# A fused attention and three-convolution kernel: mask products ahead of the first convolution, a longer TensorE loop, and the third convolution's end on ScalarE and GpSimd

## The chip, the cores and the metric

One core of a Trainium2 chip runs the whole program. The metric is the device time of one execution in microseconds. Three timed executions of the kernel before took 2295.17 (the median), 2292.28 and 2295.76 us.

## The reference, cut to what matters

The input x is [8, 128, 128, 64] in float32 (NHWC). A local attention over the 3x3 neighbourhood of each pixel comes first, then three 3x3 convolutions with ReLU, and the sum of the attention's output and the convolutions' output is returned:

```python
q = einsum('bhwd,de->bhwe', x, Q_P)
k = einsum('bhwkd,de->bhwke', stk, K_P)        # stk: the 9 shifted views of x
v = einsum('bhwkd,de->bhwke', stk, V_P)
alpha = softmax(einsum('bhwke,bhwe->bhwk', k, q) * mask)
t = x + einsum('bhwk,bhwke->bhwe', alpha, v)
t_in = t
t = relu(conv(t, ff1_kernel) + ff1_bias)        # 64 -> 64
t = relu(conv(t, ff2_kernel) + ff2_bias)        # 64 -> 128
t = relu(conv(t, ff3_kernel) + ff3_bias)        # 128 -> 64
return t_in + t
```

## The kernel before, in words

Images are worked on in 4 pairs (PAIRS), an image in each half of the 128 partitions. An image is cut into 16 bands of 8 rows (BANDS). One **step** works on one band at several stages at once: attention of band b, and the three convolutions of the bands behind it. A pair has 17 steps, k = 0 to 16; step k = 15 has no attention part (att is False), since the next pair's first band is taken up in k = 16. There are 68 steps, and the tail behind them finishes the last piece of the third convolution.

**Attention of a band.** TensorE makes r = (Q K^T) x for all 16 patches of 8x8 pixels (r_product, L367 to L374, into mix_bank and proj_bank). ScalarE copies r to rq (keep_r, L639). For each half of the patches TensorE makes scores: first four bfloat16 matmuls put the window mask (0 or a very negative number) into score_banks (L387), then 16 small products per half add the scores on top (L393). VectorE takes the maxima (max_scores, L756), ScalarE the exponentials (L627), VectorE scales by the reciprocal sum (scale, L762 and L765), TensorE turns the probabilities (turn, L405), ScalarE copies them (keep_turned, L644), TensorE multiplies them with x (mix, L420), ScalarE copies the result (keep_y, L634), TensorE applies V (v_product, L432), and VectorE adds x and writes tf (add_x, L776).

**Convolutions.** Each is done in a transformed domain with four streams, in which the column direction costs four products for two outputs. VectorE prepares the inputs from the ReLU's output (transform, L789, L790, L794), TensorE multiplies (conv1 L442, conv3_tile L484, begin2, go_on2 and end2 L500), ScalarE copies one of the two middle streams out of PSUM (keep_m2, L663, and keep_u2, L651), VectorE forms sum and difference with the other (middle and middle1, L819 to L833) and then adds the two outer streams (outer, outer1, outer3: L866, L841, L857). ScalarE adds bias and ReLU for convolutions 1 and 2 (L679, L693). For the third convolution VectorE does all of it: the bias goes in with middle (L819, L820), and finish (L783) takes the maximum with 0 and adds the kept attention output, in one scalar_tensor_tensor. SyncE then stores the band (store, L317).

**Order.** The order on every engine is written out by hand as a fixed sequence of calls per step. The functions schedule (for SyncE, ScalarE and VectorE) and the loop at L610 (for TensorE) run it: a loop over the pairs holds k = 0 and k = 1 written out, then an inner loop, then the last steps written out. TensorE's inner loop has 12 rounds (k = 2 to 13), and k = 14, 15, 16 are written out behind it. GpSimd has no loop: it only zeroes buffers and prepares the weights of the third convolution at the start. At the end of a step TensorE runs end2(G, k, 2) and end2(G, k, 3); the second has a wait for the next band inside it (await_band, L362), in every step but k = 14. The next step opens with r_product and then the inner half of conv1, which waits for outer of the second convolution's odd rows (L866) on VectorE, for dt_done, and for the small copy of dt.

**SyncE** issues all transfers in a fixed order per step: the copy of dt, loads of xs and xc, copies of dodd and deven, the store, the load of xk behind a wait for mix, the load of xr behind add_x, six copies into kept, and the copies of duh and dul behind the last tile of the second convolution.

Of the kernel before, what the change touches and what calls it, by code (L numbers as in the profile page):

```python
# [61 lines left out]
def pairs3(k):  # L62
    return (2, RP) if k == 1 else (0, 2) if k == 0 else (0, RP)
# [11 lines left out]
def build(nc, x_bands, x_keys, qt2, kt, vbd, w1, w2, w3, b1, b2, b3, window, eye, eye16, out):  # L75
    with ExitStack() as ctx:
# [6 lines left out]
        def sem(name):  # L83
            return ctx.enter_context(nc.semaphore(name))
# [91 lines left out]
        dve_read = sem("dve_read")  # L176
        sum_done = sem("sum_done")
        relu_done = sem("relu_done")
        dt_done = sem("dt_done")
        du_high = sem("du_high")  # L180
        du_low = sem("du_low")
# [175 lines left out]
        def _(pe):  # L357
# [20 lines left out]
                if half:  # L378
                    pe.wait_ge(probt_ready, b * 2 + 1)

            def scores(b, half):
                banks = [score_banks[:, n, 0:GROUP * KEYS].rearrange("q (a n) -> q a n", n=KEYS) for n in range(2)]
                mask = window_sb[:].rearrange("q (o n) -> q o n", o=1).broadcast_to([128, GROUP, KEYS])
                for n, swap in ((0, False), (1, True)):
                    for rows in (LOWER, UPPER):
                        to = (UPPER if rows is LOWER else LOWER) if swap else rows
                        nc.tensor.matmul(banks[n][to], eye16_sb[rows, rows], mask[rows], start=True, stop=False)  # L387
                for a in range(GROUP):
                    for n, swap in ((0, False), (1, True)):
                        patch = half * HALF + n * GROUP + a  # L390
                        for rows in (LOWER, UPPER):
                            to = (UPPER if rows is LOWER else LOWER) if swap else rows
                            mm = nc.tensor.matmul(banks[n][to, a], rq[rows, patch],  # L393
                                                  xc[rows, :, patch * PATCH:patch * PATCH + HALO],
                                                  start=False, stop=a == GROUP - 1)
                            if a == GROUP - 1:
                                mm.then_inc(scores_done, 1)
# [152 lines left out]
            r_product(0)  # L550
            await_r(0, 0)
            hold(score_banks[:, 0])
            scores(0, 0)
            await_prob(0, 0)
            hold(score_banks[:, 0])
            turn(0, 0)
            await_r(0, 1)
            hold(score_banks[:, 0])
            scores(0, 1)
            mix(0, 0)  # L560
            await_prob(0, 1)
# [11 lines left out]
            def step(G, k, b, att):  # L573
                if att:
                    r_product(b)
                conv1(G, k, b, False, att)
                if att:
                    scores(b, 0)
                conv1(G, k, b, True)
                conv3_tile(G, k, 0)  # L580
                conv3_tile(G, k, 1, (lambda: await_prob(b, 0)) if att else None)
                if att:
                    turn(b, 0)
                conv3_tile(G, k, 2, (lambda: await_r(b, 1)) if att else None)
                if att:
                    scores(b, 1)
                conv3_tile(G, k, 3)
                if att:
                    mix(b, 0)
                begin2(G, k, 0)  # L590
                go_on2(G, k, 0)
                begin2(G, k, 1, (lambda: await_prob(b, 1)) if att else None)
                if att:
                    turn(b, 1)
                go_on2(G, k, 1)
                end2(G, k, 0)
                end2(G, k, 1)
                if att:
                    mix(b, 1)
                begin2(G, k, 2, (lambda: await_y(b)) if att else None)  # L600
                if att:
                    v_product(b)
                go_on2(G, k, 2)
                begin2(G, k, 3)
                go_on2(G, k, 3)
                end2(G, k, 2)
                next_band = None if k == BANDS - 2 else b if k == BANDS - 1 else b + 1
                end2(G, k, 3, None if next_band is None else lambda: await_band(next_band))

            with pe.Fori(0, PAIRS) as p:  # L610
                g0, b0 = p * STEPS, p * BANDS
                step(g0, 0, b0 + 1, True)
                step(g0 + 1, 1, b0 + 2, True)
                with pe.Fori(0, BANDS - 4) as h:
                    step(g0 + h + 2, 2, b0 + h + 3, True)
                step(g0 + (BANDS - 2), BANDS - 2, b0 + (BANDS - 1), True)
                step(g0 + (BANDS - 1), BANDS - 1, b0 + BANDS, False)
                step(g0 + BANDS, BANDS, b0 + BANDS, True)
            for j in range(4):
# [3 lines left out]
        def _(act):  # L623
# [60 lines left out]
            def relu_conv2(G, k, which, behind=0):  # L684
# [6 lines left out]
                if k == BANDS and which == EVEN:  # L691
                    nc.scalar.copy(to[:, 1, :, 1:1 + W], zeros[:, 0])
                nc.scalar.activation(to[:, lo:hi, :, 1:1 + W], sums[which][:, lo:hi], ACT.Relu,  # L693
                                     bias=bias[:, 1:2]).then_inc(relu_done, 1)

            def u_high(G, k, part):
                act.wait_ge(d_done[CONV1], parts(G, part))
                if part == 0:
                    act.wait_ge(u_kept, G * 32 + 32)
                streams, n = PARTS[part], new_slots(CONV1, k)  # L700
                nc.scalar.copy(duh[:, 1:n + 1, streams], du[:, 0:n, streams]).then_inc(du_high, 1)
# [15 lines left out]
            def step(G, k, b, par, att):  # L717
                if att:
                    keep_r(b, 0)
                if k:  # L720
                    relu_conv2(G, k - 1, ODD, 1)
                    relu_conv2(G, k - 1, EVEN, 1)
                if att:
                    keep_r(b, 1)
                keep_u2(G, k)
                if att:
                    exps(b, 0)
                    exps(b, 1)
                keep_m2(G, k, CONV3)
                relu_conv1(G, k)  # L730
                if att:
                    keep_turned(b, 0)
                u_high(G, k, 0)
                u_high(G, k, 1)
                if att:
                    exps(b, 2)
                    exps(b, 3)
                if att:
                    keep_y(b, 0)
                    keep_turned(b, 1)  # L740
                keep_m2(G, k, ODD)
                keep_m2(G, k, EVEN)
                if att:
                    keep_y(b, 1)
                if k == BANDS:
                    relu_conv2(G, k, ODD)
                    relu_conv2(G, k, EVEN)

            schedule(act, step)
            keep_m2(ALL_STEPS, 0, CONV3)  # L750

        @block.vector
        def _(dve):
# [13 lines left out]
            def add_x(k, b, par, i):  # L767
# [6 lines left out]
                v = (proj_bank, mix_bank)[i][:].rearrange("c (a r s) -> c r a s", r=RP, s=PATCH)  # L774
                x = xr[:, :, i].rearrange("c r (a s) -> c r a s", s=PATCH)
                nc.vector.tensor_tensor(o, v, x, ALU.add).then_inc(t_ready, 1)  # L776

            def finish(G, k, b):
                lo, hi = pairs3(k)
                dve.wait_ge(dve_read, outer_read(G, CONV3))  # L780
                dve.wait_ge(carried, carries(k, b))
                o = sums[CONV3][:, lo:hi]
                nc.vector.scalar_tensor_tensor(o, o, 0.0, kept[:, k % 2 if k else 1, lo:hi], ALU.max,  # L783
                                               ALU.add).then_inc(out_ready, 1)

            def transform(to, src, slots, part, done):
                if part == 0:
# [21 lines left out]
            def middle(G, k, which):  # L809
                lo, hi = pairs(which, k)  # L810
                bank = conv_banks[:, bank_of(which, 1)].rearrange("c (s i w) -> c s i w", i=2, w=WT)
                m1, m2 = bank[:, lo:hi], m2_sb[:, which % 2, lo:hi]
                left, right = (sums[which][:, lo:hi, :, n::2] for n in range(2))
                dve.wait_ge(act_read, act_reads(G, which))
                dve.wait_ge(tile_done, filled(G, which, 1))
                if which == CONV3:
                    dve.wait_ge(sent, G * 16 + 16)
                if which == CONV3:
                    nc.vector.scalar_tensor_tensor(left, m1, bias[:, 2:3], m2, ALU.add, ALU.add)  # L819
                    nc.vector.scalar_tensor_tensor(right, m1, bias[:, 2:3], m2, ALU.add,  # L820
                                                   ALU.subtract).then_inc(dve_read, 1)
                else:
                    nc.vector.tensor_tensor(left, m1, m2, ALU.add)
                    nc.vector.tensor_tensor(right, m1, m2, ALU.subtract).then_inc(dve_read, 1)

            def middle1(G, k):
                lo, hi = pairs1(k)
# [75 lines left out]
            def step(G, k, b, par, att):  # L903
# [32 lines left out]
                    scale(b, 2)  # L936
                    scale(b, 3)
                u_low(G, k, 1)
                finish(G, k, b)
                middle(G, k, ODD)  # L940
                middle(G, k, EVEN)
                if att:
# [10 lines left out]
            schedule(dve, step)  # L953
            middle(ALL_STEPS, 0, CONV3)
            outer3(ALL_STEPS, 0)
            finish(ALL_STEPS, 0, PAIRS * BANDS + 1)

        @block.gpsimd
        def _(pool):
# [8 lines left out]
                nc.gpsimd.memset(credits[:, i:i + 1], 0.0).then_inc(credit, n)  # L968
            pool.wait_ge(w_in, 80)
            whole_weights(nc.gpsimd, pool.wait_ge, raws[3], w3f, half3, w3_stage).then_inc(w_ready, 1)  # L970


# [79 lines left out]
```

## Time and profile before

| | |
|---|---|
| profiled execution, its own time | 2292.98 us |
| its span | 2291.0 us |
| granted TensorE clock, mean | 0.987 |
| PE busy | 2184.0 us (95%) |
| VectorE (DVE) busy | 1894.3 us (83%) |
| ScalarE (ACT) busy | 1132.7 us (49%) |
| GpSimd (POOL) busy | 15.5 us (1%) |

Busy time is a union over an engine's instructions. PE is TensorE's matmuls and PEld its weight loads, which overlap the matmuls. Every matmul on float32 appears as two records. A busy PE is not PE at its peak, since matmuls are pipelined and their ends are modelled. The chain of waits goes back from the last instruction to what released each one, so what stands in it sets the end.

### The profile page before, as it was taken

The page shows a single profiled execution, that of the slowest core. Times are in us where ns is not written, and L with a number is a line of the kernel's source. Part 1 is how long each engine was busy: PE and PEld are TensorE (multiplying, and loading weights), DVE is VectorE, ACT ScalarE, POOL GpSimd, SP SyncE. Part 2 cuts the span into 40 slices and gives each one's busy share as a digit, 9 for nine tenths or more (in the row PEclk, how much of TensorE's full clock was granted, in tenths as well). Part 3 has the DMA queues.
Part 4 walks back from the last instruction along what each step waited for, and adds up shares of the span by engine and source line. Part 5 has one row for each costly group of instructions (what it writes and reads, how often), then busy time and mean ns, then how long its engine had stood idle before and what let it go on. Part 6 is the DMA issues. An engine that isn't in the chain of part 4 may idle for free.

```text
span 2291.0 us, 63881 instructions
## 1 busy us (share of the span) xinstructions
PE 2184.0 (95%) x24401; PEld 1222.3 (53%) x24401; DVE 1894.3 (83%) x2850; ACT 1132.7 (49%) x3108; POOL 15.5 (1%) x24
## 2 busy tenths in 40 slices
PE   4999999999899999999989999999988999999998
PEld 2555555554455555555455555555545555555554
DVE  4888888888688888888768888888876888888885
ACT  2555455553455455455345555555434555554542
POOL 2000000000000000000000000000000000000000
PEclk8999999999999999999999999999999999999999
DMA  5454544554355444544345445445534544454444
GB/s 130 140 145 142 166 141 136 155 153 136 103 155 168 145 140 147 161 145 132 118 145 154 136 154 156 145 132 166 151 117 111 168 146 142 139 166 145 141 147 124
DMA packets 291284, 328.75 MB, mean 144 GB/s; under 512 B 89300, under 2 KB 223252, under 8 KB 284564
## 3 DMA queue, kind: packets, MB, share of 16 engines
q1 hardware_dynamic: 291164, 327.17, 48.2%
q8 instruction: 73, 1.20, 0.2%
q14 instruction: 47, 0.39, 0.1%
HBM read 152.50 MB, written 33.82 MB: 81 GB/s over the span
## 4 chain that ended last, share of the span: by engine, by line
PE 87%; DVE 6%; issue 3%; ACT 1%; DMA 1%; SPq 1%; DVEq 0%; ACTq 0%
PE conv_banks L484 29%; PE conv_banks L500 24%; PE conv_banks L442 17%; PE mix_bank L420 5%; PE score_banks L393 4%; DVE work L866 3%; PE score_banks L405 3%; PE mix_bank L432 3%; PE score_banks L387 1%; DMA work<-w 1%; ACT probt L644 1%; DVE prob L765 0%; PE mix_bank L372 0%; ACT prob L627 0%; DVE tf L776 0%
## 5 line engine op out<-in xcount | busy, mean ns | idle before, releaser
L484 PE MATMUL conv_banks<-dodd,w3f 128*64 128x512 f32 (+1 forms) x1656 | 503.5, 582 | 11.9 <-DVE work L833 9.2
L484 PE MATMUL conv_banks<-deven,w3f 128*64 128x512 f32 (+1 forms) x1656 | 496.3, 570 | 8.7 <-DVE prob L765 7.0
L627 ACT ACTIVATE prob<-score_banks,negmax 128x100 f32<-128x100 f32 x1040 | 343.0, 343 | 195.4 <-DVE negmax L756 195.4
L442 PE MATMUL conv_banks<-dt,w1f 128*64 128x256 f32 (+3 forms) x4224 | 413.9, 384 | 22.3 <-DVE work L866 22.3
L442 PEld LDWEIGHTS conv_banks<-dt,w1f 128*64 128x64 f32 (+1 forms) x4224 | 219.2, 135 | 235.9 <-DVE work L866 83.4
L500 PE MATMUL conv_banks<-duh,w2h 64*128 64x512 f32 (+2 forms) x1632 | 327.6, 399 | 4.0 <-ACT m_sb L663 2.1
L500 PE MATMUL conv_banks<-duh,w2l 64*128 64x512 f32 (+2 forms) x1632 | 319.3, 388 | 6.0 <-DVE prob L765 5.2
L500 PE MATMUL conv_banks<-dul,w2h 64*128 64x512 f32 (+2 forms) x1632 | 282.4, 396 | 0.9 <-DVE tf L776 0.9
L484 PEld LDWEIGHTS conv_banks<-dodd,w3f 128*64 128x64 f32 x1656 | 138.0, 137 | 236.4 <-issue 212.0
L644 ACT COPY probt<-score_banks 100x1024 f32<-100x1024 f32 x130 | 131.8, 1014 | 235.0 <-PE score_banks L405 235.0
L484 PEld LDWEIGHTS conv_banks<-deven,w3f 128*64 128x64 f32 x1656 | 155.1, 138 | 158.8 <-issue 114.6
L639 ACT COPY rq<-mix_bank 128x512 f32<-128x512 f32 x65 | 38.2, 587 | 391.1 <-PE mix_bank L372 391.1
L756 DVE TENSOR_REDUCE negmax<-score_banks 128x4 f32<-128x400 f32 x260 | 148.5, 572 | 97.1 <-PE score_banks L393 96.5
L627 ACT ACTIVATION_READ_ACCUMULATOR prob<-score_banks,negmax 128x1 f32 x1040 | 212.2, 204 | 0.0
L693 ACT ACTIVATE relued<-work,bias 128x1024 f32<-128x1024 f32 (+2 forms) x136 | 149.6, 1103 | 92.5 <-DVE work L866 92.5
L866 DVE TENSOR_TENSOR work<-conv_banks,work 128x1024 f32<-128x1024 f32 (+2 forms) x136 | 157.5, 1163 | 44.0 <-PE conv_banks L500 44.0
L500 PEld LDWEIGHTS conv_banks<-dul,w2h 64*128 64x128 f32 x1632 | 143.5, 185 | 75.2 <-issue 53.4
L663 ACT COPY m_sb<-conv_banks 128x512 f32<-128x512 f32 (+3 forms) x205 | 108.1, 562 | 146.0 <-PE conv_banks L484 107.2
L500 PEld LDWEIGHTS conv_banks<-duh,w2l 64*128 64x128 f32 x1632 | 153.6, 185 | 49.8 <-ACT rq L634 15.1
L500 PEld LDWEIGHTS conv_banks<-duh,w2h 64*128 64x128 f32 x1632 | 153.2, 184 | 47.5 <-ACT m_sb L663 3.9
L420 PEld LDWEIGHTS mix_bank<-probt,xk 100*64 100x64 f32 x4160 | 139.4, 139 | 58.0 <-issue 56.8
L806 DVE TENSOR_TENSOR dul<-work,duh 128x1024 fp32r<-128x1024 f32 (+1 forms) x136 | 159.1, 1170 | 0.0
(93 smaller groups left out, 2937.6 us busy)
## 6 DMA issues: line engine op xcount, KB each, us to landing
xk<-x_keys SPq DMA_DIRECT2D x66, 800.0 KB
xc<-x_bands SPq DMA_DIRECT2D x66, 650.0 KB, 5.0
dodd<-dodd SPq DMA_DIRECT2D x68, 512.0 KB, 5.1
xr<-x_bands SPq DMA_DIRECT2D x264, 128.0 KB, 3.5
out<-work SPq DMA_DIRECT2D x60, 512.0 KB, 2.7
dt<-dt SPq DMA_DIRECT2D x68, 256.0 KB, 2.3
deven<-deven SPq DMA_DIRECT2D x68, 256.0 KB, 5.6
duh<-duh SPq DMA_DIRECT2D x68, 256.0 KB, 2.4
```

Source lines behind the costliest of these rows:

```text
L393: mm = nc.tensor.matmul(banks[n][to, a], rq[rows, patch], xc[rows, :, patch * PATCH:patch * PATCH + HALO], start=False, stop=a == GROUP - 1)
L420: last = nc.tensor.matmul(mix_bank[image, a * C:(a + 1) * C], xk[:, patch, image], probt[:, half, i if a < GROUP else 1 - i, a], start=Tru ...
L442: mm = nc.tensor.matmul(bank[(LOWER, UPPER)[o], n * 256 + lo * 64:n * 256 + hi * 64], w1f[i][rows, m, s, o * C:o * C + C], dt[rows, lo + s ...
L484: return nc.tensor.matmul(bank[rows, lo * 128:hi * 128], w3f[:, m, s, odd * C:odd * C + C], source[:, lo + s // 2:hi + s // 2, m], start=s ...
L500: return nc.tensor.matmul(conv_banks[:, bank_of(which, j), lo * 128:hi * 128], w[rows, STREAMS[j], 2 * (which == EVEN) + s], d[rows, lo + ...
L627: last = nc.scalar.activation(prob[:, g % 2, a], score_banks[:, g % 2, a * KEYS:(a + 1) * KEYS], ACT.Exp, bias=negmax[:, g % 2, a:a + 1], ...
L644: nc.scalar.copy(probt[:, half], score_banks[0:KEYS].rearrange("n i (a q) -> n i a q", q=C)).then_inc(probt_ready, 1)
L663: nc.scalar.copy(m2_sb[:, which % 2, lo:hi], bank[:, lo:hi]).then_inc(act_read, 1)
L693: nc.scalar.activation(to[:, lo:hi, :, 1:1 + W], sums[which][:, lo:hi], ACT.Relu, bias=bias[:, 1:2]).then_inc(relu_done, 1)
L756: nc.vector.tensor_reduce(negmax[:, g % 2], score_banks[:, g % 2, 0:GROUP * KEYS].rearrange("q (a n) -> q a n", n=KEYS), AX_X, ALU.max, ne ...
L806: nc.vector.tensor_tensor(dul[:, 1:n + 1, streams], du[:, 0:n, streams], duh[:, 1:n + 1, streams].bitcast(F32), ALU.subtract).then_inc(du_ ...
L866: nc.vector.tensor_tensor(both, m03, both, ALU.add).then_inc(dve_read, 1)
```

## The change: what it does

**Mask products.** The four mask matmuls leave the function scores and become masks(). For the first half of the patches they are issued right behind r_product, ahead of conv1; for the second half they stay where they were, ahead of scores(b, 1).

**TensorE's loop.** The inner loop has 13 rounds (k = 2 to 14); only k = 15 and 16 are written out behind it. The wait for the next band is now in step k = 14 as well.

**The third convolution's end.** middle of the third convolution becomes a plain sum and difference without bias. finish leaves VectorE. ScalarE gets relu_conv3, an activation with the bias in place, behind keep_y(b, 1) near the end of its step; GpSimd gets a loop with one tensor_tensor per step, which adds kept. The store waits for GpSimd.

```diff
+            banks = [score_banks[:, n, 0:GROUP * KEYS].rearrange("q (a n) -> q a n", n=KEYS) for n in range(2)]
+
+            def masks():
                 mask = window_sb[:].rearrange("q (o n) -> q o n", o=1).broadcast_to([128, GROUP, KEYS])
                 for n, swap in ((0, False), (1, True)):
                     for rows in (LOWER, UPPER):
                         to = (UPPER if rows is LOWER else LOWER) if swap else rows
                         nc.tensor.matmul(banks[n][to], eye16_sb[rows, rows], mask[rows], start=True, stop=False)
+
+            def scores(b, half):
...
                 if att:
                     r_product(b)
+                    masks()
                 conv1(G, k, b, False, att)
...
                 conv3_tile(G, k, 2, (lambda: await_r(b, 1)) if att else None)
                 if att:
+                    masks()
                     scores(b, 1)
...
-                next_band = None if k == BANDS - 2 else b if k == BANDS - 1 else b + 1
-                end2(G, k, 3, None if next_band is None else lambda: await_band(next_band))
+                end2(G, k, 3, lambda: await_band(b + 1 if att else b))
...
-                with pe.Fori(0, BANDS - 4) as h:
+                with pe.Fori(0, BANDS - 3) as h:
                     step(g0 + h + 2, 2, b0 + h + 3, True)
-                step(g0 + (BANDS - 2), BANDS - 2, b0 + (BANDS - 1), True)
                 step(g0 + (BANDS - 1), BANDS - 1, b0 + BANDS, False)
...
+            def relu_conv3(G, k):                                  # ScalarE
+                lo, hi = pairs3(k)
+                act.wait_ge(dve_read, outer_read(G, CONV3))
+                o = sums[CONV3][:, lo:hi]
+                nc.scalar.activation(o, o, ACT.Relu, bias=bias[:, 2:3]).then_inc(relu3_done, 1)
...
                 if att:
                     keep_y(b, 1)
+                relu_conv3(G, k)
                 if k == BANDS:
                     relu_conv2(G, k, ODD)
...
-                if which == CONV3:                                 # VectorE, middle
-                    nc.vector.scalar_tensor_tensor(left, m1, bias[:, 2:3], m2, ALU.add, ALU.add)
-                    nc.vector.scalar_tensor_tensor(right, m1, bias[:, 2:3], m2, ALU.add,
-                                                   ALU.subtract).then_inc(dve_read, 1)
-                else:
-                    nc.vector.tensor_tensor(left, m1, m2, ALU.add)
-                    nc.vector.tensor_tensor(right, m1, m2, ALU.subtract).then_inc(dve_read, 1)
+                nc.vector.tensor_tensor(left, m1, m2, ALU.add)
+                nc.vector.tensor_tensor(right, m1, m2, ALU.subtract).then_inc(dve_read, 1)
...
                 u_low(G, k, 1)
-                finish(G, k, b)
                 middle(G, k, ODD)
...
+            def finish(G, k, b):                                   # GpSimd
+                lo, hi = pairs3(k)
+                pool.wait_ge(relu3_done, G + 1)
+                pool.wait_ge(carried, carries(k, b))
+                o = sums[CONV3][:, lo:hi]
+                nc.gpsimd.tensor_tensor(o, o, kept[:, k % 2 if k else 1, lo:hi], ALU.add).then_inc(out_ready, 1)
+
+            def step(G, k, b, par, att):
+                finish(G, k, b)
+
+            schedule(pool, step)
+            finish(ALL_STEPS, 0, PAIRS * BANDS + 1)
```

The tail changes in the same way: ScalarE's relu_conv3(ALL_STEPS, 0) and GpSimd's finish stand in place of VectorE's finish.

## Rows read from the trace of the kernel before

**Rows 1.** Page, chain that ended last: share of the span by engine.

```profile
PE 87%; DVE 6%; issue 3%; ACT 1%; DMA 1%; SPq 1%; DVEq 0%; ACTq 0%
```

**Rows 2.** The chain over one step's start: start us, us, what, pieces.

```profile
999.60 1.24 DVE work L866
...
1000.88 2.97 PE conv_banks L442 x32
1003.85 0.17 PE score_banks L387 x4
```

**Rows 3.** Busy time by engine in that whole step, start of conv1 to the next.

```profile
1000.88:1033.94 33.06, 32.78 (x368) 18.14 (x368) 28.83 (x43) 17.26 (x48) 0.00 (x0) 1.00 0.49 147
```

**Rows 4.** Timeline of PE there: start, length, matmuls merged, idle time before.

```profile
999.94 0.66 PE L372 MATMUL mix_bank<-xc,qk 64*64 64x512 f32 x2
1000.88 0.44 PE L442 MATMUL conv_banks<-dt,w1f 128*64 128x256 f32 x2 [0.28 <-DVE work L866]
...
1003.67 0.35 PE L387 MATMUL score_banks<-window_sb,eye_sb 64*64 64x400 bf16 x4
```

**Rows 5.** Timeline of PE, PEld, DVE at the first probabilities' wait.

```profile
1011.47 1.02 PE L484 MATMUL conv_banks<-deven,w3f 128*64 128x512 f32 x3
1011.66 0.38 PEld L484 LDWEIGHTS conv_banks<-deven,w3f 128*64 128x64 f32 x4 [0.48 <-DVE prob L765]
1011.03 0.57 DVE L765 TENSOR_TENSOR prob<-prob,expinv 128x400 f32<-128x400 f32 x1
```

**Rows 6.** Timeline of DVE in a step k = 1.

```profile
1205.42 1.23 DVE L841 TENSOR_TENSOR work<-conv_banks,work 128x1024 f32<-128x1024 f32 x1 [0.22 <-PE conv_banks L442]
```

**Rows 7.** Timeline of PE where a pair of images ends (three such places).

```profile
1161.61 1.12 PE L372 MATMUL mix_bank<-xc,qk 64*64 64x512 f32 x2 [3.93 <-issue]
...
1723.03 1.11 PE L372 MATMUL mix_bank<-xc,qk 64*64 64x512 f32 x2 [6.64 <-issue]
```

**Rows 8.** Timeline of ACT, then DVE, at the end of a step.

```profile
993.84 0.59 ACT L634 COPY rq<-mix_bank 128x512 f32<-128x512 f32 x1 [0.65 <-PE mix_bank L420]
1000.67 0.59 ACT L639 COPY rq<-mix_bank 128x512 f32<-128x512 f32 x1 [6.25 <-PE mix_bank L372]
1001.16 1.16 ACT L693 ACTIVATE relued<-work,bias 128x1024 f32<-128x1024 f32 x1
...
996.31 0.69 DVE L776 TENSOR_TENSOR tf<-mix_bank,xr 128x512 f32<-128x512 f32 x1 [1.01 <-PE proj_bank L432]
997.72 0.69 DVE L789 TENSOR_TENSOR dt<-tf 128x512 f32<-128x512 f32 x1
998.33 0.69 DVE L790 TENSOR_TENSOR dt<-tf 128x512 f32<-128x512 f32 x1
999.60 1.23 DVE L866 TENSOR_TENSOR work<-conv_banks,work 128x1024 f32<-128x1024 f32 x1 [0.58 <-PE conv_banks L500]
```

**Rows 9.** Page, costliest groups: finish on VectorE (busy, mean ns, idle before).

```profile
L783 DVE SCALAR_TENSOR_TENSOR work<-work,kept 128x1024 f32<-128x1024 f32 (+1 forms) x69 | 79.2, 1148 | 0.0
```

**Rows 10.** Timeline of POOL, then DVE, while both prepare weights.

```profile
26.82 1.49 POOL L251 TENSOR_TENSOR work<-work 128x512 f32<-128x512 f32 x1 [20.21 <-DMA work<-w]
28.39 1.32 POOL L253 TENSOR_TENSOR w3f<-work 128x512 f32<-128x512 f32 x1
...
27.23 1.37 DVE L253 TENSOR_TENSOR w1f<-work 128x256 f32<-128x256 f32 x1
...
33.00 0.43 DVE L253 TENSOR_TENSOR w1f<-work 128x256 f32<-128x256 f32 x1
```

**Rows 11.** Timeline of SP's issues around the end of that step.

```profile
993.97 0.32 SPq L276 DMA_DIRECT2D xk<-x_keys  x1
...
1007.76 0.47 SPq L321 DMA_DIRECT2D dt<-dt  x1
```

**Rows 12.** The last piece of the chain, then ACT's timeline near it.

```profile
2287.81 0.69 DVE work L783
...
2278.22 0.51 ACT L693 ACTIVATE relued<-work,bias 128x256 f32<-128x256 f32 x1 [4.79 <-DVE work L866]
```

More of the change, by code:

```diff
@@ L178, in build @@
         relu_done = sem("relu_done")
+        relu3_done = sem("relu3_done")
         dt_done = sem("dt_done")
@@ L379, in await_r @@
                     pe.wait_ge(probt_ready, b * 2 + 1)
-            def scores(b, half):
-                banks = [score_banks[:, n, 0:GROUP * KEYS].rearrange("q (a n) -> q a n", n=KEYS) for n in range(2)]
+            banks = [score_banks[:, n, 0:GROUP * KEYS].rearrange("q (a n) -> q a n", n=KEYS) for n in range(2)]
+            def masks():
                 mask = window_sb[:].rearrange("q (o n) -> q o n", o=1).broadcast_to([128, GROUP, KEYS])
@@ L575, in step @@
                     r_product(b)
+                    masks()
                 conv1(G, k, b, False, att)
@@ L585, in step @@
                 if att:
+                    masks()
                     scores(b, 1)
@@ L750, in _ @@
             keep_m2(ALL_STEPS, 0, CONV3)
+            relu_conv3(ALL_STEPS, 0)
         @block.vector
@@ L776, in add_x @@
                 nc.vector.tensor_tensor(o, v, x, ALU.add).then_inc(t_ready, 1)
[L778 to L784, printed above, removed]
             def transform(to, src, slots, part, done):
@@ L955, in _ @@
             outer3(ALL_STEPS, 0)
-            finish(ALL_STEPS, 0, PAIRS * BANDS + 1)
         @block.gpsimd
```

## The prediction

> **What bounds the kernel now.** I read the chain of waits first, by engine: 87% of the span lies on PE and 6% on DVE [rows 1]. Then I read the chain and the busy times over one step, to see what a step consists of. From one start of conv1 to the next it is 33.06 us, of which PE is busy 32.78 and VectorE 28.83 [rows 3]. TensorE is the bound, so a microsecond taken off VectorE's busy time is worth nothing by itself. The one place of the step where the chain leaves PE is its seam: behind end2 VectorE's outer sum L866 runs from 999.60 to 1000.84, and conv1 starts at 1000.88 [rows 2]. In that hole TensorE already has r_product, whose last matmuls run until 1000.60, and then it is idle for 0.28 us by the timeline [rows 4]. The mask matmuls lie elsewhere, behind conv1's first half, and there they are on the chain with 0.17 us for the four [rows 2]. Their first record is at 1003.67, and their 0.35 us overlap the scores that follow [rows 4].
>
> A second thing is to be read before counting. VectorE works without a break from 999.60 to the end of the scaling L765 at 1011.03 + 0.57 = 1011.60, and TensorE's weight load in conv3_tile 1 waits for just that: it starts at 1011.66 [rows 5]. So a second path runs beside TensorE's, from L866 over VectorE to this load, and it has next to no slack.
>
> **The masks.** Nothing is removed: four matmuls move in front of conv1, into the hole. They need score_banks free, and mix(b-1, 1), long issued, has waited for the last reader of it. Each lasts 0.35 us by its record but only 0.17 us pass before the next matmul may start. Behind r_product (its last start is 999.94, and 0.43 us later the array is free, by the beat of equally long f32 matmuls worked out below) they run from about 1000.4 to 1000.6 or 1000.7, and conv1 can't start before 1000.88. They cost 0 there and 0.17 us goes away behind conv1. If the hole were gone they would cost the same 0.17 again.
>
> How much arrives depends on the second path. The row of L484 at 1011.47 merges three matmuls in 1.02 us, of which the last is 0.59 long (as its kind is), so the beat is 0.43 and the matmuls for which the load is made start at 1011.90 [rows 5]. The load is from 1011.66 and takes 0.14 (four merged: 0.38), so it is ready at 1011.80 if all of it must be over, 0.10 ahead; if the array needs only its beginning, it is 0.24 ahead at most. So per step between 0.10 and 0.17 us arrives. I take the 0.17: exposed loads in this trace start together with their matmul (conv1's at 1000.88), not 0.14 ahead of it.
>
> It counts in k = 2 to 14, where conv1's starts are 33.05 to 33.06 apart by the timeline, and in k = 1, where the second path is behind TensorE too (VectorE idles 0.22 us for conv1 ahead of L841 [rows 6]), so that it moves along. In k = 0 the time before conv1 is TensorE's own, k = 16 is held by VectorE throughout, k = 15 has no masks. That is 14 x 4 = 56 steps: 56 x 0.17 = 9.5 us less (low end 52 x 0.10 + 4 x 0.17 = 5.9).
>
> **The loop.** Step k = 14 issues the same instructions from the loop's body instead of from its own copy. The wait for the next band is new there. Behind it on TensorE are the last matmuls of end2 and, in k = 15, conv1. It waits for add_x, whose first half starts at 996.31 and whose second follows at once [rows 8], and for loads issued before the store, so 0 us, as in the twelve rounds that have it already. What could move is the hole at the end of a pair, where TensorE fetches the beginning of the outer loop: 3.93 us twice and 6.64 once, put down to issue [rows 7]. That jump is the same before and after; I take 0, with bounds of 3 x 2.71 = 8.1 us more and 2.7 us less (the long one becoming short).
>
> **VectorE without finish.** 69 instructions of 1.15 us go [rows 9], and the two middle sums lose their bias operand. Behind finish VectorE idles anyway until TensorE and ScalarE deliver the next tiles, so it is worth 0. Its next late moment is the L866 at 999.60, which waits 0.58 us for TensorE [rows 8].
>
> **ScalarE's ReLU.** It is issued behind keep_y(b, 1), which ends at 994.43; ScalarE is then idle for 6.25 us until keep_r [rows 8]. The same shape takes 1.16 us there, so it ends at 995.6. Cost 0; only the 4.7 us left are used up if that cover goes.
>
> **GpSimd's addition.** The trace has no GpSimd addition of 1024 elements and none beside the loop's VectorE work. The nearest rows are the weights' preparation [rows 10]. GpSimd's L251 ends at 28.31 and VectorE's L253, which began at 27.23 and takes 0.43 alone, ends at 28.60; GpSimd's L253 then ends at 29.71, 1.11 us behind that. The two take turns, each held for the whole of the other. So 512 elements cost GpSimd 1.11 us when it has its turn, and 1024 some 2.2; the high end is 2 x 1.49 = 3.0. Started at 995.65, it ends at 997.9 (998.65). VectorE's additions with both inputs in SBUF wait: L789 should start at 997.72. Held until 997.9 it ends 0.29 + 0.26 = 0.55 us later (from the 0.29 by which L253 ended behind GpSimd, and the 0.26 that 512 elements take longer than 256), at 998.4, as before. At the high end L790 ends at 999.8 and L866 is 0.1 us late, 5.6 us over 56 steps. I take 0. A lucky order can't bring a gain, since L866 waits for TensorE.
>
> The Trainium skill ("SBUF — State Buffer", who interferes with whom) says that GpSimd and VectorE share one port pair under an exclusive lock, which a VectorE instruction takes when it has two SBUF inputs. By that rule add_x, with one input in PSUM, runs freely; the rows of the weights agree for two SBUF inputs, and none shows the other kind. Its "GPSIMD Engine Reference" (performance versus the Vector engine) gives 4497 ns for 2048 elements, an estimate of 2.25 us for 1024; the sum would be the same.
>
> **SyncE.** The store now waits for 997.9, and xk's load behind it, before at 993.97, goes out at about 998.4. xr's four, which wait for add_x, follow it, and what is behind them moves by about 1 us, down to the copy of dt, which is at 1007.76 now [rows 11] and may be 0.5 us later. xk is read by the next step's mix, in the second half of its 33 us, and dt's copy by add_x's followers at that step's end. Cost 0.
>
> **The tail.** The last finish, 0.69 us [rows 12], becomes ScalarE's ReLU over 512 elements (between 0.51 for 256 and 1.16 for 1024, about 0.7), GpSimd's 1.1 to 1.5 and one more hand-over of 0.1: +1.2 to +1.6; in the last step's end L789 may be held 0.25 on the chain. I take +1.5.
>
> **Sum.** -9.5 + 1.5 = -8.0 us, on the profiled execution's own 2292.98 (span 2291.0): 2285.0. The median shown lies 2.2 above that execution, so I forecast 2287.2 against 2295.17. A difference under 0.2% (4.6 us) can't be told from none.
>
> **The rivals.**
>
> (A) The second path takes its share: the load must be whole before its matmuls, and the masks yield 5.9 less 1.5, 4.4 us: 2290.8. For it: the load's start is VectorE's, 0.05 us behind L765. Against it: conv1's exposed load.
>
> (B) The other side: GpSimd's turn also holds additions with one PSUM input. Then add_x, due at 996.31, is held to 997.9; it ends at 998.4, its second half at 999.05, L789 and L790 at 999.8 and 1000.4, and L866 starts at 1000.3 instead of 999.60. That is 0.7 us in 56 steps, 39 us: 2326. It decides from the point where GpSimd ends later than 998.55, or holds add_x at all. For it: an instruction of 0.43 took 1.37 beside GpSimd [rows 10]. Against it: that one had both inputs in SBUF. With only some of it (GpSimd's 3.0 us) the time is 2293.
>
> (C) The loop's new length changes TensorE's fetching: all three holes at 6.64 give +5.4, 2292.6; short ones -2.7.
>
> (D) The change gives more than I count: VectorE's relief speeds the uneven steps k = 15, 16, 0, 1, where it is often the releaser. Ten moments in each pair at which it releases TensorE 0.1 us earlier would be 4 us: 2283.2.
>
> **How the numbers follow.** My forecast 0.56, A 0.18, B 0.10 (half of it near 2293, half near 2326), C 0.09, D 0.07. Faster by over 0.2% means below 2290.6: nearly all of the forecast, D, and a third of A, 0.66 rounded down to 0.64 for what isn't seen; same 0.27; slower 0.09, B's harder half and some of C and of the unseen. The range goes from 2282 (D, with the runs' own 1 to 3 us) to 2295 (A, C and the mild B).
>
> **What would show it.** The step from k = 2 to 14 becomes 32.89 us (A: 32.96; B: over 33.7). The mask matmuls stand between r_product and conv1, whose start is still 1.28 us behind L866's. L866 is still preceded by an idle time of about 0.5 us that ends with TensorE. GpSimd's addition lasts 2.2 us and starts 1.8 us behind keep_y's start, and L789 starts or lasts longer by 0.1 to 0.2. The weight load at 1011.66 waits longer than 0.48 and its matmuls keep their beat. Pair ends keep holes of 4 to 7 us. I am wrong if the step isn't shorter, or if L866 waits for L790.

## The result, and the profile after

The changed kernel takes 2308.67 us (median of 6 executions, 2307.67 to 2311.29) against 2293.73 for the kernel before (median of 6), a ratio of 1.0065 with a 95% interval of 1.0052 to 1.0077. It is 15 us slower; 2287.2 was forecast, in a range that ended at 2295. The profiled spans are 2305.7 and 2291.0 us.

The page of the changed kernel: engine totals, the main DMA queue (packets, MB, share of 16 engines' time), and the chain by engine [rows 1].

```profile
PE 2199.9 (95%) x24401; PEld 1231.2 (53%) x24401; DVE 1815.5 (79%) x2781; ACT 1202.5 (52%) x3177; POOL 170.9 (7%) x93
...
q1 hardware_dynamic: 291164, 327.17, 55.3%
...
PE 84%; DVE 7%; issue 5%; ACT 2%; DMA 1%; SPq 1%; DVEq 0%; POOL 0%; ACTq 0%; POOLq 0%
```

VectorE has 79 us less to do, and it bought nothing. The chain's share of issue, time in which an engine waits for nothing that the profile shows, went from 3% to 5%, and the same 327.17 MB took 55.3% of the DMA engines' time where the page of before has 48.2%.

Read step by step (from one start of conv1 to the next), the loss isn't where the loop is. The step that answers to [rows 3]:

```profile
1006.08:1039.04 32.96, 32.85 (x368) 18.25 (x368) 27.62 (x42) 18.31 (x49) 2.40 (x1) 1.00 0.59 148
```

It is shorter, 32.96 us instead of 33.06, in all 52 steps k = 2 to 14. The three steps k = 0 that begin a later pair are another matter: 40.9, 41.0 and 40.9 us instead of 33.8, 34.9 and 34.1. In the first of them, the timeline of ScalarE and then of VectorE:

```profile
601.33 0.39 ACT L698 COPY relued<-zeros 128x256 f32<-128x256 f32 x1
601.62 0.51 ACT L699 ACTIVATE relued<-work,bias 128x256 f32<-128x256 f32 x1
609.77 0.59 ACT L645 COPY rq<-mix_bank 128x512 f32<-128x512 f32 x1 [7.64 <-issue]
...
602.96 0.68 DVE L800 TENSOR_TENSOR deven<-relued 128x512 f32<-128x512 f32 x1
610.64 1.23 DVE L800 TENSOR_TENSOR dt<-tf 128x1024 f32<-128x1024 f32 x1 [6.99 <-issue]
```

The same places of before:

```profile
602.01 0.50 ACT L693 ACTIVATE relued<-work,bias 128x256 f32<-128x256 f32 x1
606.02 0.58 ACT L639 COPY rq<-mix_bank 128x512 f32<-128x512 f32 x1 [3.51 <-PE mix_bank L372]
...
606.49 1.23 DVE L794 TENSOR_TENSOR dt<-tf 128x1024 f32<-128x1024 f32 x1 [2.46 <-issue]
```

Before, ScalarE was ready first and waited for TensorE's r. After, r is there and ScalarE doesn't start for 7.64 us, put down to issue: it is at the jump back to the beginning of its outer loop. VectorE stands at its own jump for 6.99 us instead of 2.46. TensorE pays for it in conv1, which needs rq for its second half. Timeline of PE after:

```profile
604.63 0.58 PE L389 MATMUL score_banks<-window_sb,eye_sb 64*64 64x400 bf16 x4
605.14 1.91 PE L446 MATMUL conv_banks<-dt,w1f 128*64 128x256 f32 x12
610.41 7.24 PE L446 MATMUL conv_banks<-dt,w1f 128*64 128x256 f32 x19 [3.35 <-ACT rq L645]
```

Its 31 matmuls need 1.91 and 7.24 us with a wait of 3.35 between them (by the modelled ends). Before, they ran in one piece:

```profile
605.91 6.26 PE L442 MATMUL conv_banks<-dt,w1f 128*64 128x256 f32 x31
```

So 3.35 us are the wait, and 1.91 + 7.24 - 6.26 = 2.89 come from a slower TensorE. The windows over the second part after, and over the second part before (columns as in [rows 3]; the granted clock stands before the DMA share):

```profile
610.41:617.65 7.24, 7.24 (x30) 3.04 (x31) 1.23 (x1) 0.44 (x1) 0.00 (x0) 0.50 0.30 76
```

```profile
608.00:612.00 4.00, 4.00 (x26) 1.82 (x25) 0.00 (x0) 0.00 (x0) 0.00 (x0) 1.00 0.43 149
```

0.50 is the lower level, 1.2 GHz, and 1.00 the upper, 2.4 GHz. Before, TensorE worked without a break from the end of the hole at its own jump (604.00; [rows 7] has two other such holes); its granted clock was 0.56 from 605.91 to 608 and 1.00 from there. After, it had begun to rise in conv1's first part (0.78 as the mean from 605.14 to 607.05); then TensorE stood idle for 3.35 us, and all of the second part runs at the lower level. The 0.9 us that are left of this step's 7.1 lie behind it, where the clock is still low (0.58 from 617.65 to 620; before it is 1.00 from 612 to 616).

What do the DMA engines do meanwhile? SyncE's issues around that place, after:

```profile
599.57 0.37 SPq L318 DMA_DIRECT2D out<-work  x1
600.22 0.32 SPq L277 DMA_DIRECT2D xk<-x_keys  x1
600.72 3.11 SPq L282 DMA_DIRECT2D xr<-x_bands  x4
603.87 1.96 SPq L287 DMA_DIRECT2D kept<-tf  x3
```

and before:

```profile
594.32 0.37 SPq L317 DMA_DIRECT2D out<-work  x1
596.05 0.32 SPq L276 DMA_DIRECT2D xk<-x_keys  x1
599.67 3.07 SPq L281 DMA_DIRECT2D xr<-x_bands  x3
```

The store waits for GpSimd and went out 5 us later; xk's 800 KB stand behind it in SyncE's order and went with it. Now the queues of the DMA engines in a stretch of 4.4 us from ScalarE's last work before the jump (packets, MB, share of 16 engines' time). Before, 601.7 to 606.1:

```profile
q1 hardware_dynamic: 1287, 0.61, 58.1%
q8 instruction: 1, 0.02, 2.9%
q14 instruction: 3, 0.02, 1.4%
```

After, 601.3 to 605.7:

```profile
q1 hardware_dynamic: 369, 0.91, 85.1%
q8 instruction: 1, 0.02, 2.1%
```

Three packets of queue 14 bring instructions before, none after (queue 8 has one in both). From 605.7 to 609.7, after:

```profile
q1 hardware_dynamic: 996, 0.74, 105.2%
q14 instruction: 2, 0.02, 1.9%
```

Only in this stretch do they come, and ScalarE starts at its end, at 609.77. The theory to be tested, T: the late transfers fill the DMA engines at the moment at which ScalarE and VectorE fetch the beginning of their loops. The rival, R: the restart is late because GpSimd has a loop of its own now and ScalarE's program is longer.

### The profile page after: what moved, and what is told of

Its sections match the earlier page's. It is cut to its first block, busy times and chain, and to the rows that moved or that the text cites. A ratio compares the mean times of both kernels' runs of the same rounds, so it can differ in the third digit from the quotient of the medians.

```text
span 2305.7 us, 64103 instructions
## 1 busy us (share of the span) xinstructions
PE 2199.9 (95%) x24401; PEld 1231.2 (53%) x24401; DVE 1815.5 (79%) x2781; ACT 1202.5 (52%) x3177; POOL 170.9 (7%) x93
## 3 DMA queue, kind: packets, MB, share of 16 engines
q1 hardware_dynamic: 291164, 327.17, 55.3%
## 4 chain that ended last, share of the span: by engine, by line
PE 84%; DVE 7%; issue 5%; ACT 2%; DMA 1%; SPq 1%; DVEq 0%; POOL 0%; ACTq 0%; POOLq 0%
PE conv_banks L488 28%; PE conv_banks L504 24%; PE conv_banks L446 16%; PE mix_bank L424 5%; PE score_banks L397 4%; DVE work L867 4%; PE score_banks L409 3%; PE mix_bank L436 3%; PE score_banks L389 1%; DMA work<-w 1%; ACT probt L650 1%; DVE prob L779 0%; DMA kept<-tf 0%; DVE negmax L770 0%; ACT relued L699 0%
## 5 line engine op out<-in xcount | busy, mean ns | idle before, releaser
L446 PE MATMUL conv_banks<-dt,w1f 128*64 128x256 f32 (+3 forms) x4224 | 423.8, 386 | 21.2 <-ACT rq L645 9.3
L976 POOL TENSOR_TENSOR work<-work,kept 128x1024 f32<-128x1024 f32 (+1 forms) x69 | 155.4, 2252 | 2111.4 <-ACT work L706 2098.5
L824 DVE TENSOR_TENSOR work<-conv_banks,m_sb 128x512 f32<-128x512 f32 (+3 forms) x205 | 135.2, 660 | 136.6 <-PE conv_banks L504 119.4
L867 DVE TENSOR_TENSOR work<-conv_banks,work 128x1024 f32<-128x1024 f32 (+2 forms) x136 | 157.7, 1164 | 35.3 <-PE conv_banks L504 35.3
```

The costliest lines, as they stand in the source:

```text
L446: mm = nc.tensor.matmul(bank[(LOWER, UPPER)[o], n * 256 + lo * 64:n * 256 + hi * 64], w1f[i][rows, m, s, o * C:o * C + C], dt[rows, lo + s ...
L867: nc.vector.tensor_tensor(both, m03, both, ALU.add).then_inc(dve_read, 1)
L976: nc.gpsimd.tensor_tensor(o, o, kept[:, k % 2 if k else 1, lo:hi], ALU.add).then_inc(out_ready, 1)
```

## The experiments

Each was timed beside the kernel before on the same chip. Steps are from one start of conv1 to the next in its trace.

**e1_store_behind_loads**, the change with another order on SyncE:

```diff
-                store(G, k)
                 if att:
                     sp.wait_ge(mixed, b * 2 + 2)
                     load_xk(b + 1)
                     sp.wait_ge(t_ready, b * 2 + 2)
                     load_xr(b + 1)
+                store(G, k)
```

> The changed kernel with SyncE's order altered in every step: the loads of xk and xr go out on their old conditions (behind mix and add_x) and the store, which waits for GpSimd, follows them. All else is the change. Theory T (transfers at the end of a pair): at a pair's end the late store and the load of xk behind it fill the DMA engines just when ScalarE and VectorE fetch the beginning of their outer loop; with xk out by 596 again, step k = 0 of the later pairs goes from 40.9 back to 34 to 35.5 us and the kernel takes 2285 to 2290 us. Rival R (programs): the restart is late because GpSimd now has a loop of its own and ScalarE's program is longer; SyncE's order doesn't matter, k = 0 stays at 40 to 41 us and the time at 2306 to 2310.

Measured: 2283.96 us against 2292.78, ratio 0.9968 (0.9957 to 0.9979). The steps k = 0 are 34.6, 34.0 and 34.6 us. R falls: GpSimd's loop and ScalarE's program are all there. ScalarE at its jump:

```profile
602.88 0.51 ACT L699 ACTIVATE relued<-work,bias 128x256 f32<-128x256 f32 x1
606.47 0.59 ACT L645 COPY rq<-mix_bank 128x512 f32<-128x512 f32 x1 [3.08 <-PE mix_bank L373]
```

**e2_vector_finish**, the kernel before with the masks and the loop of the change only.

> The kernel before with the mask products behind r and the longer TensorE loop, the third convolution's end left on VectorE. Both theories: 2285 to 2289 us, with steps k = 2 to 14 at 32.9 to 33.0 us and k = 0 of the later pairs at 33.5 to 35. If k = 0 is 40 us here too, the masks or the loop are to blame and both theories fall.

Measured: 2283.23 against 2292.78, ratio 0.9964 (0.995 to 0.9978), 2 us below the range expected. Steps k = 2 to 14 are 32.90 to 32.97, k = 0 33.4 to 33.6, so neither the masks nor the loop is to blame.

**e3_conv3_end_alone**, the kernel before with the third convolution's end of the change only.

> The kernel before with the third convolution's end on ScalarE and GpSimd, and nothing else of the change: the masks stay in scores and TensorE's loop keeps 12 rounds. Both theories: 20 us more from three steps k = 0 and 1 to 2 us from the tail, 2312 to 2317 us, steps k = 2 to 14 at 33.05. A third view, that masks ahead of conv1 in k = 0 cause part of the loss, expects less than 2308.

Measured: 2312.35 against 2292.78, ratio 1.0094 (1.0077 to 1.0111). The steps of the loop are 33.07: taking 1.1 us off VectorE there (27.72 us busy in a step instead of 28.83) neither helps nor hurts. Two of the three steps k = 0 are 41.4 and 41.7 us, but one, the second, is 35.5, where both theories expected a long one. In that place ScalarE starts again 5.01 us after its last work, with TensorE (whose own hole is 4.93 us there) as the releaser, and VectorE after 5.43. The first instruction packet came earlier than in the change, though not as early as before: from 1169.7, ScalarE's jump, to 1175 the queues have

```profile
q1 hardware_dynamic: 582, 1.17, 79.6%
q14 instruction: 1, 0.01, 0.6%
```

That packet starts at 1173.4. So how long the fetch is held differs from one pair's end to the next in this kernel.

**e5_late_store_pair_end**, the kernel before with nothing altered but SyncE's order in k = 16:

```diff
-                store(G, k)
-                if att:
-                    sp.wait_ge(mixed, b * 2 + 2)
+                if att and k == BANDS:
+                    sp.wait_ge(t_ready, b * 2 + 2)
+                    sp.dma_start(out[:, G, lo:hi], sums[CONV3][:, lo:hi]).then_inc(sent, 16)
                     load_xk(b + 1)
-                    sp.wait_ge(t_ready, b * 2 + 2)
                     load_xr(b + 1)
+                else:
+                    ...
```

> The kernel before, with VectorE's finish, and only SyncE's order altered and only in step k = 16: the store, and the load of xk behind it, wait for add_x, as late as GpSimd's addition makes them in the changed kernel. Theory T: this alone makes k = 0 of the later pairs 39 to 41 us long, 2308 to 2314 us. Rival R: no GpSimd loop, no longer ScalarE program, so 2292 to 2296 us.

Measured: 2311.42 against 2292.78, ratio 1.0086 (1.0069 to 1.0102), steps k = 0 of 41.2, 40.3 and 41.2. This is the loss by itself, without one instruction of the computing engines altered. ScalarE and SyncE in it:

```profile
605.45 0.51 ACT L700 ACTIVATE relued<-work,bias 128x256 f32<-128x256 f32 x1
614.79 0.59 ACT L646 COPY rq<-mix_bank 128x512 f32<-128x512 f32 x1 [8.84 <-issue]
...
603.13 0.37 SPq L332 DMA_DIRECT2D out<-work  x1
603.68 0.32 SPq L276 DMA_DIRECT2D xk<-x_keys  x1
604.18 3.26 SPq L281 DMA_DIRECT2D xr<-x_bands  x4
```

**e6_loop_alone**, the kernel before with TensorE's longer loop only.

> The kernel before with only TensorE's inner loop longer by one step (and the wait for the next band in it). Theory: nothing on the path changes, steps k = 2 to 14 stay at 33.06 us and the time within 3 us of before. Rival: a part of the gain of the kernel with masks and loop (9.6 us) comes from the loop, by shorter restarts of TensorE at a pair's end; then 2288 to 2291 us, with the holes ahead of r_product near 3.6 us in all three places instead of 3.9, 3.9 and 6.6.

Measured: 2292.6 against 2293.38, ratio 0.9996 (0.9987 to 1.0006): no difference. The steps stay at 33.06 us; the three holes are 3.8, 3.5 and 4.0 us, with no gain in the time.

**e8_loads_next_pair**, the change with the two loads of k = 16 moved to the next pair (and the same two of the prologue to the first pair's k = 0), the store as late as in the change:

```diff
             def step(G, k, b, par, att):
+                if k == 0:
+                    load_xk(b)
+                    load_xr(b)
                 sp.wait_ge(conv1_done, G * 8 + 8)
...
-                if att:
+                if att and k < BANDS:
                     sp.wait_ge(mixed, b * 2 + 2)
                     load_xk(b + 1)
```

> The changed kernel, store as late as it is there, but in step k = 16 the loads of xk and xr (1312 KB) aren't issued; they go out at the beginning of the next pair's k = 0, behind SyncE's own jump. Theory T (transfers): with them away from the place where ScalarE and VectorE fetch their instructions, k = 0 of the later pairs goes from 40.9 to at most 34.5 us though the store stays late: 2278 to 2288 us. Rival (the late store itself, or GpSimd's loop, delays the fetch): k = 0 stays above 38 us, 2300 to 2310.

Measured: 2282.97 against 2293.38, ratio 0.9948 (0.9931 to 0.9964), steps k = 0 of 33.5, 34.6 and 33.3. The store went out at 601.16 here, 1.7 us before ScalarE's jump at 602.9 (in the change 599.57, with the jump at 601.3), and did no harm; the loads, 1312 KB, are what stood in the way. The rival falls with both its halves.

**e10_xk_first_at_pair_end**, the change with the load of xk ahead of the store, in k = 16 alone.

> The changed kernel with one exchange, in step k = 16 alone: the load of xk goes out ahead of the store, as soon as mix is done, and xr behind the store. Steps k = 0 to 15 are the change's. Theory T: 800 KB that were in front of the instruction fetch are moved to where the DMA engines idled (594 to 599 in the changed kernel); k = 0 of the later pairs falls from 40.9 to 33.5 to 36 us and the time is 2282 to 2289 us. Rival (each late store delays something in every step, so that the order of one step can't give it back): over 2300 us.

Measured: 2284.15 against 2292.19, ratio 0.9964 (0.995 to 0.9978), steps k = 0 of 33.2 to 33.8. One exchange, ahead of three jumps, takes 24 us off the change's 2308.67 (the two were timed in different sets of runs) and gives back all that it lost. The late stores of the other steps cost nothing. It also says which load: the store (600.90) and the first of xr's loads (601.46) still go out 2.1 and 1.5 us ahead of ScalarE's last work at 602.96 (in the change 2.1 and 0.9), and only xk, 800 KB, is gone from there.

The DMA packets in the twelve traces say the same. xk's load is 100 packets of 8 KB. In the change they begin within 0.2 us of the end of ScalarE's last work and run for 5.2 to 5.7 us, and the first packet of queue 14 follows the start of the last of them by 0.04 to 0.25 us. Over all 36 pair ends, that first packet starts 2.9 to 5.9 us after ScalarE's last work in the nine where the first packet of xk's load starts within 0.6 us of it (the change, e3, e5), and within 1.2 us in the other 27. VectorE starts again 1.3 to 2.3 us after the end of queue 14's second packet in all 36: when the packet is late, the engine is late by as much.

But T's wording, that the transfers "fill" the engines, is too simple. At the third pair end of e1, the 4.4 us from 1712.05 have

```profile
q1 hardware_dynamic: 1226, 1.01, 92.9%
q14 instruction: 2, 0.02, 1.5%
```

More bytes and a larger share than the 85.1% of the change, and yet the instructions come in time and k = 0 takes 34.6 us. What the slow places have in common is that xk's load begins just then, not a high share.

**e7_middle_first**, e2 with an exchange on VectorE, for the masks' missing part:

```diff
-                if att:
-                    max_scores(b, 0)
                 middle1(G, k)
                 if att:
+                    max_scores(b, 0)
                     max_scores(b, 1)
```

> The kernel with masks and loop and VectorE's finish (e2_vector_finish), with one exchange on VectorE: middle1 ahead of max_scores(b, 0), so that conv3_tile 0 is released some 0.5 us earlier. Theory: the masks yield only 0.11 of their 0.17 us in k = 2 to 14 because conv3_tile 0 then waits for middle1; with the exchange steps k = 2 to 14 go from 32.93 to 32.88 us and the kernel to 2279 to 2282 us. Rival: the probabilities (scale, later by the exchange) hold TensorE instead, and the steps stay or grow by up to 0.5 us (2283 to 2310).

Measured: 2274.72 against 2293.38, ratio 0.9917 (0.99 to 0.9934). The step is

```profile
999.13:1032.02 32.89, 32.78 (x369) 18.17 (x369) 28.71 (x43) 17.18 (x48) 0.00 (x0) 1.00 0.48 149
```

The step behaved as expected (32.93 to 32.88), the time did not: more came. Between the traced executions of e2 and e7, 6.0 us apart in span, the 52 steps give 2.4 us. The three stretches k = 16 and next k = 0 give 3.8, of which the wait ahead of conv3_tile 0 in k = 16 (2.25 us in e2, now 1.77) explains 1.4. The last step with the tail gives 1.9, and the start of the program takes 2.0 back. The medians of e2 and e7 are 8.5 us apart, but each was timed beside other runs of the kernel before, and e2's traced execution was its fastest by 2.6 us. What makes up the remainder stays open.

**e9_middle_and_loads**, e7 with the loads of k = 16 moved as in e8.

> Masks and loop, VectorE's finish, middle1 ahead of max_scores(b, 0), and the loads of xk and xr of k = 16 moved to the beginning of the next pair's k = 0: the version that should beat both. Theory T: the holes at a pair's end come partly from transfers in the kernel before too (3.9, 3.9 and 6.6 us), so they shrink below 3.5, and together with the exchange the time is 2272 to 2279 us. Rival: the holes are the fetch's own latency and stay at 3.5 us or more: 2279 to 2283 us.

Measured: 2274.73 against 2293.38, ratio 0.9918 (0.9901 to 0.9934), the same as e7. TensorE's holes at a pair's end are 3.7, 4.1 and 3.4 us. So T's extension falls: the time lies in its range, but the holes didn't shrink below 3.5 us, and the gain is e7's. In the order of before the transfers delay nothing, and 3.4 to 4.1 us is what that jump costs TensorE anyhow.

**e11_all_best**, e1 with e7's exchange: ScalarE and GpSimd make the end, the store is behind the loads.

> The changed kernel with the store behind the loads in every step and middle1 ahead of max_scores(b, 0) on VectorE: ScalarE and GpSimd still make the third convolution's end. Theory: VectorE's relief is worth nothing, so it is 0 to 2 us slower than the same version with VectorE's finish (e7_middle_first, 2274.7): 2274 to 2278 us, steps k = 2 to 14 at 32.89. Rival: with the exchange VectorE is nearer to TensorE's path and its 1.3 us less per step now pay: 2268 to 2273 us.

Measured: 2275.64 against 2292.19, ratio 0.9929 (0.9912 to 0.9945), steps of 32.87 to 32.90. It is no faster than e7: with VectorE 1.1 us emptier in every step, nothing changes. e7 and e11 beat both kernels, the one before by 0.8 and 0.7%.

## Why the prediction was wrong, point by point

**SyncE: this step failed.** The prediction had the store and xk's load go out some 4.5 us later, and they did. It priced that by who reads the data (xk by the next step's mix, dt's copy by add_x's followers) and wrote "Cost 0". It didn't ask what else uses the DMA engines in the stretch into which the transfers move. At the end of a pair that is the instruction fetch of ScalarE and VectorE. Priced there: k = 0 of three pairs 7.1, 6.1 and 6.8 us longer, 20 us. e5 shows that the late transfers alone do it, e8 that it is the loads and not the store, e10 that moving xk's load undoes it. That the instruction packets come late, and the engines with them, is seen in the packets' times. Why they come late with xk's 8 KB packets in flight, and not with as many bytes of other transfers, is not shown: no run varies the packets' size, and none shows the order within an engine.

**The loop: the right question, the wrong answer.** The prediction named the hole at a pair's end and took "That jump is the same before and after". It looked at TensorE's jump alone, which got no longer (3.4, 3.2 and 4.1 us after). The 6.64 us of the third place did not come back, here or in any other run; that accounts for 2.5 of the 2.6 us by which k = 16 is shorter in sum, and it was the prediction's bound of 2.7 us less, not its forecast. e6 has short holes too and no gain in its median, so this may be the chance of one execution. ScalarE and VectorE jump there too. Before, VectorE's row of that place already read 2.46 us of issue, the sign that a fetch is exposed, and none of the rows I chose shows it. Rival C (5.4 us, and 8.1 in the bound, which counts the already long hole once more) was about TensorE's fetch, and too small. The longer loop itself: 0, right (e6).

**The masks: the mechanism right, the size too large.** They stand in the hole and cost nothing there: after, the timeline of PE has

```profile
1038.11 0.66 PE L373 MATMUL mix_bank<-xc,qk 64*64 64x512 f32 x2
1038.49 0.45 PE L389 MATMUL score_banks<-window_sb,eye_sb 64*64 64x400 bf16 x4
1039.04 0.44 PE L446 MATMUL conv_banks<-dt,w1f 128*64 128x256 f32 x2
```

The scores start 0.16 us earlier behind conv1's start (1008.88 - 1006.08 = 2.80; before 2.96), but the step is 0.07 to 0.13 shorter: 32.95 on average, rival A's sign (32.96) and not the forecast's 32.89. Rival A was right that a second path over VectorE takes a share, and put it at the wrong place: not at the probabilities' wait (the matmul there keeps its beat), but at the first tile of the third convolution, 4 us earlier, which waits for middle1. VectorE, then PE, after:

```profile
1011.83 0.68 DVE L834 TENSOR_TENSOR work<-conv_banks,m_sb 128x512 f32<-128x512 f32 x1
...
1012.65 0.65 PE L488 MATMUL conv_banks<-dodd,w3f 128*64 128x512 f32 x2
```

That is 6.57 us behind conv1's start at 1006.08. Before it was 6.67, and 0.17 less would be 6.50. In e7 it is

```profile
1005.62 1.50 PE L487 MATMUL conv_banks<-dodd,w3f 128*64 128x512 f32 x5
```

6.49 behind 999.13, and the whole 0.17 arrives. So the term was 5.5 us in k = 2 to 14 and 0.7 in k = 1, 6.2 instead of 9.5.

**VectorE without finish: right, 0** (e11 against e7, e3's steps). **ScalarE's ReLU: right**: 1032.48 and 1.15 us, with 5.20 us idle behind it.

**GpSimd's addition: right.** Timeline of POOL, then DVE, after [rows 8, 10]:

```profile
1033.82 2.40 POOL L976 TENSOR_TENSOR work<-work,kept 128x1024 f32<-128x1024 f32 x1 [30.57 <-ACT work L706]
...
1034.50 0.69 DVE L790 TENSOR_TENSOR tf<-mix_bank,xr 128x512 f32<-128x512 f32 x1 [1.04 <-PE proj_bank L436]
1035.91 0.86 DVE L795 TENSOR_TENSOR dt<-tf 128x512 f32<-128x512 f32 x1
1037.76 1.22 DVE L867 TENSOR_TENSOR work<-conv_banks,work 128x1024 f32<-128x1024 f32 x1 [0.40 <-PE conv_banks L504]
```

2.40 us against 2.2 estimated. add_x, with one input in PSUM, runs in its old 0.69 beside it; L795, with both inputs in SBUF, takes 0.86 instead of 0.69, held by GpSimd, which ended at 1036.22: it ends 0.55 us behind that, the 0.29 + 0.26 of the prediction. L867 still waits 0.40 us for TensorE. Rival B is out. The Trainium skill ("SBUF — State Buffer", who interferes with whom) has the lock just so, and the trace agrees for both kinds of input: 0.69 us with one input in PSUM, 0.86 with two in SBUF.

**The tail: +1.5 forecast.** From the last step's conv1 to the end it is 46.0 us after and 43.3 before, +2.6. ScalarE's last ReLU ended at 2300.62, but GpSimd's last addition starts at 2301.93 and waits for a copy into kept, which had been put back with the store:

```profile
2301.93 1.26 POOL L976 TENSOR_TENSOR work<-work,kept 128x512 f32<-128x512 f32 x1 [12.93 <-DMA kept<-tf]
```

With the loads first (e1) GpSimd doesn't wait for that copy, and the stretch is 43.3 us; against the 41.7 of e2, which has VectorE's finish, that is +1.7, near the +1.5 forecast.

**The sum, as it came, in spans:** k = 0 of three pairs +20.0, k = 2 to 14 -5.5, k = 1 -0.7, k = 16 -2.6, tail +2.6, the first steps +0.8: 14.6 of 14.7 us.

**A near hit that is luck.** e1, the change without its loss, is 8.8 us faster than the kernel before, where the sum had -8.0. The masks gave some 6.4 of the 9.5 us counted (k = 1 to 14); the rest is made up elsewhere, above all in k = 16, in its traced execution 6.1 us shorter over three pairs, which was not forecast. That VectorE's relief is its source, as rival D had it, is ruled out by e11 against e7.

## What to carry to other kernels

A transfer that moves in time is to be priced twice: by who reads its data, and by what else the DMA engines must carry where it lands. Where loops jump, instructions are among that, and their delay shows as idle time "issue" on engines that seem to have time to spare. The DMA engines' busy share doesn't tell whether they are delayed; the times of the instruction queue's packets do. A store that waits for a slower producer holds back every load behind it in the same queue: put the loads first, and look at the queue's order again after every change of who finishes last.

## What the runs showed of the hardware that was not expected

At the jump back over the outer loop ScalarE began again 2.7 to 3.7 us after its last work (6.2 once), released by TensorE by then, and VectorE after 1.5 to 3.0, in the 27 pair ends at which xk's load came earlier or later. With that load beginning at the jump, ScalarE took 6.2 to 8.8 us and VectorE 6.2 to 7.8 (5.0 and 5.4 once), in programs that are otherwise alike (e5 against before). At the jumps of the inner loops no such hole shows on TensorE (steps k = 2 to 14 are 33.05 to 33.06 before), and none put down to issue on ScalarE or VectorE.

The DMA engines' time for the same 327.17 MB differs with the order of issue: 48.2% before, 55.3% in the change, 47.9% in e1; xr's load took 3.5 us to land before and 7.5 in the change. This is another effect than the loss: e10 has 55.4% and is fast, e5 has 47.7% and is slow. In a step of the loop it was free.
